# Mixing of a pair behind the next unit's scores, projections in front of both transposes: attention and feed-forward block on one core

## What is computed

```python
xn = layernorm(x)
q, k = rope(q, k)                       # q: 32 heads, k and v: 8 heads of 64
scores = einsum('bgrtd,bgsd->bgrts', q, k) / sqrt(64)
allowed = (j <= i) & (i - j < 128)
attn = softmax(where(allowed, scores, -inf))
out = einsum('bgrts,bgsd->bgrtd', attn, v)  @ Wo
ffn: fwht, W_up and W_gate, silu(gate) * up, fwht, W_down
return x + attention(xn) + ffn(xn)
```

## Time and profile before

| | us |
|---|---|
| median of 3 runs | 1280.19 (1279.04 to 1281.07) |
| the profiled execution | 1279.16 |
| span of its profile | 1277.4 |
| PE busy | 1251.5 (98%) |
| DVE busy | 904.4 (71%) |
| ACT busy | 779.6 (61%) |
| POOL busy | 644.0 (50%) |
| granted PE clock | 1.0 throughout |

### The profile page before, as it was taken

How to read it: one execution, slowest core, us unless ns; L and a number is a source line. 1 busy time by engine, 2 the same in 40 slices (tenths; PEclk the granted TensorE clock), 3 DMA queues, 4 the chain that set the end, 5 groups by cost and what they waited for, 6 DMA issues and landing times.

```text
span 1277.4 us, 38064 instructions
## 1 busy us (share of the span) xinstructions
PE 1251.5 (98%) x14574; PEld 1062.3 (83%) x14574; DVE 904.4 (71%) x1617; ACT 779.6 (61%) x2862; POOL 644.0 (50%) x655
## 2 busy tenths in 40 slices
PE   9999999999999999999999999999999999999997
PEld 5778888888888888878888888888888888888886
DVE  5678974788647885478855888458884588746875
ACT  3377762767528775377744867357672667626775
POOL 5346652466426654266641766327663376524663
PEclk9999999999999999999999999999999999999999
DMA  6415535144152442334332343314424145141431
GB/s 224 124 47 163 173 110 149 53 127 138 35 149 78 114 127 76 108 85 143 92 98 84 109 132 95 112 55 123 127 86 131 59 111 155 62 132 38 132 99 51
DMA packets 72354, 137.56 MB, mean 108 GB/s; under 512 B 15600, under 2 KB 29424, under 8 KB 72176
## 3 DMA queue, kind: packets, MB, share of 16 engines
q1 hardware_dynamic: 71040, 134.41, 35.1%
q10 hardware_dynamic: 1136, 0.73, 0.2%
HBM read 72.17 MB, written 12.58 MB: 66 GB/s over the span
## 4 chain that ended last, share of the span: by engine, by line
PE 82%; ACT 6%; SPq 4%; DVE 3%; DMA 2%; issue 2%; POOL 1%; DVEq 0%; POOLq 0%
PE PROJ L964 15%; PE PROJ L966 14%; PE PROJ L965 14%; PE S L1120 10%; PE TR L1134 8%; PE O L1151 5%; PE O L1163 4%; PE TR L1151 4%; ACT e_sb L643 4%; PE S L964 2%; SPq L397 2%; PE S L965 2%; PE S L966 2%; DMA q_stack<-qy 1%; SPq L387 1%
## 5 line engine op out<-in xcount | busy, mean ns | idle before, releaser
L643 ACT ACTIVATE e_sb<-S,negmax 128x128 f32<-128x128 f32 x1024 | 364.8, 382 | 25.0 <-DVE negmax L888 22.6
L511 POOL TENSOR_TENSOR e_sb<-e_sb,rinv 128x512 f32<-128x512 f32 x256 | 264.8, 1040 | 49.3 <-DVE rinv L893 49.0
L519 POOL TENSOR_SCALAR_AFFINE_SELECT p_cur<-pt_sb 128x512 f32<-128x512 f32 x192 | 122.5, 641 | 246.3 <-ACT pt_sb L653 246.3
L653 ACT ACTIVATE pt_sb<-TR 128x512 f32<-128x512 f32 x256 | 154.9, 605 | 135.7 <-PE TR L1134 135.4
L773 DVE TENSOR_TENSOR prod<-PROJ,rope_sb 128x1024 f32<-128x1024 f32 x160 | 193.3, 1212 | 60.0 <-PE PROJ L966 43.3
L643 ACT ACTIVATION_READ_ACCUMULATOR e_sb<-S,negmax 128x1 f32 x1024 | 225.3, 220 | 0.0
L888 DVE TENSOR_REDUCE negmax<-S 128x4 f32<-128x512 f32 x256 | 177.1, 692 | 8.9
L1120 PE MATMUL S<-k_stack,q_stack 64*64 64x64 f32 (+2 forms) x5632 | 180.2, 266 | 1.3 <-ACT e_sb L643 1.3
L487 POOL TENSOR_TENSOR qy<-prod 128x512 f32<-128x512 f32 x64 | 82.2, 1284 | 174.4 <-DVE prod L773 162.2
L1120 PEld LDWEIGHTS S<-k_stack,q_stack 64*64 64x64 f32 x5632 | 161.7, 133 | 8.6 <-ACT e_sb L643 5.4
L637 ACT ACTIVATE staging_rest<-PROJ,scale_gu_sb 128x512 f32<-128x512 f32 x64 | 44.2, 690 | 201.1 <-PE PROJ L966 201.1
(11 more groups left out here) (105 smaller groups left out, 2900.0 us busy)
## 6 DMA issues: line engine op xcount, KB each, us to landing
q_stack<-qy SPq DMA_DIRECT2D x512, 64.0 KB, 2.1
wq_ring<-wq_split_d SPq DMA_DIRECT2D x56, 512.0 KB, 4.7
wo_ring<-wo_split_d SPq DMA_DIRECT2D x56, 512.0 KB, 3.6
k_stack<-ky SPq DMA_DIRECT2D x256, 64.0 KB, 2.8
x_in<-x SPq DMA_DIRECT2D x8, 512.0 KB, 4.5
wq_split_d<-wq_ring SPq DMA_DIRECT2D x8, 512.0 KB, 4.3
wo_split_d<-wo_ring SPq DMA_DIRECT2D x8, 512.0 KB, 3.7
out<-acc SPq DMA_DIRECT2D x16, 256.0 KB, 4.3
```

The lines of the kernel that those rows point to most:

```text
L511: nc.gpsimd.tensor_tensor(e, e, r, ALU.mult).then_inc(norm_done, 1)
L643: last = nc.scalar.activation(e_sb[:, n % 2, r, :], s_heads(n, 1)[:, r, :], ACT.Exp, bias=negmax[:, n % 2, r:r + 1], accum_out=rowsum[:, n ...
L653: nc.scalar.activation(pt_sb[:, n % 4, :, :], TR[:, :, :], ACT.Copy).then_inc(t_copied, 1)
```

## The change

Four things change together.

1. PE: the mixing of pair u-2 stands behind the scores of unit u (before, the mixing of pair u-1 stood at the end of unit u). Both fillers now stand in front of the transposes they belong to: filler 2u, transposes 2u-2, filler 2u+1, transposes 2u-1.
2. ACT, DVE and POOL follow: o_copy(u-2) is the first of ACT's unit and exps stand before the copies; both folds come before o_low; mask(2u-3) follows normalise(2u-1), and mask(2u-2) follows the rotations.
3. `e_sb`, `rowsum` and `rinv` have four buffers instead of two, `pt_sb` two instead of four. t_copy(n) now waits for the mixing of pair n/2 - 1.
4. Two tables: the projection of the next row's first k moves from slots 25, 26 to 26, 27, and a `wo` product from slot 27 to 25.

```diff
-                  ... ("k", 0, NEXT): (25, 26), ("q", 0, NEXT): (28, 30)}
+                  ... ("k", 0, NEXT): (26, 27), ("q", 0, NEXT): (28, 30)}
+    WO_SLOTS[25] = WO_SLOTS.pop(27)
...
-        e_sb = sb("e_sb", [P, 2, REP, P])
-        pt_sb = sb("pt_sb", [P, 4, REP, P])
+        e_sb = sb("e_sb", [P, 4, REP, P])
+        pt_sb = sb("pt_sb", [P, 2, REP, P])
...
# POOL
                     if u:
                         normalise(2 * u - 1)
+                    if u >= 2 and (2 * u - 3) % TT:
+                        mask(2 * u - 3)
...
-                    for n in (2 * u - 2, 2 * u - 1):
-                        if n >= 0 and n % TT:
-                            mask(n)
+                    if u and (2 * u - 2) % TT:
+                        mask(2 * u - 2)
                     if u < UNITS - 1:
                         normalise(2 * u)
+                mask(STEPS - 1)
...
# ACT, t_copy
-                    if n >= 4:
-                        act.wait_ge(pv_done, b * STEPS + n - 3)
+                    if n >= 2:
+                        act.wait_ge(pv_done, b * STEPS + n // 2 * 2)
...
# ACT, the units
-                    if u:
-                        t_copy(2 * u - 2)
+                    if u >= 2:
+                        o_copy(u - 2)
...
                         exps(2 * u)
                     read_values(2 * u)
                     if u:
-                        t_copy(2 * u - 1)
+                        t_copy(2 * u - 2)
                     if u < UNITS - 1:
                         exps(2 * u + 1)
...
                     if u:
-                        o_copy(u - 1)
+                        t_copy(2 * u - 1)
...
# DVE
                         inverse_sum(2 * u - 1)
+                    if u < UNITS - 1:
+                        fold(2 * u)
+                        fold(2 * u + 1)
                     if u >= 2:
                         o_low(b, u - 2)
...
# PE
                         scores(2 * u)
                         scores(2 * u + 1)
+                    if u >= 2:
+                        values_mixed(b, u - 2)
+                    for n in (2 * u, 2 * u + 1):
+                        fill(n)
                         if u:
-                            transposes(2 * u - 2)
-                        fill(2 * u)
-                        if u:
-                            transposes(2 * u - 1)
-                        fill(2 * u + 1)
-                    else:
-                        for n in (2 * u, 2 * u + 1):
-                            fill(n)
                             transposes(n - 2)
-                    if 1 <= u < UNITS - 1 or b == BATCH - 1 and u:
-                        values_mixed(b, u - 1)
+            values_mixed(BATCH - 1, STEPS // 2 - 1)
```

More of the change, by code:

```diff
@@ L194, in attention_and_ffn_block @@
         negmax = sb("negmax", [P, 2, REP])
-        rowsum = sb("rowsum", [P, 2, REP])
-        rinv = sb("rinv", [P, 2, REP])
-        e_sb = sb("e_sb", [P, 2, REP, P])
-        pt_sb = sb("pt_sb", [P, 4, REP, P])
+        rowsum = sb("rowsum", [P, 4, REP])
+        rinv = sb("rinv", [P, 4, REP])
+        e_sb = sb("e_sb", [P, 4, REP, P])
+        pt_sb = sb("pt_sb", [P, 2, REP, P])
         p_cur = sb("p_cur", [P, 4, REP, P])
@@ L206, in attention_and_ffn_block @@
         h_sb = [p_cur[:, n, :, :].rearrange("p r q -> p (r q)") for n in range(2)]
-        down_stage = pt_sb[:, :, :, :].rearrange("p a r q -> p (a r q)")
+        down_stage = e_sb[:, :, :, :].rearrange("p a r q -> p (a r q)")
         wd_full = down_stage.rearrange("p (f c) -> p f c", f=FT)
@@ L508, in normalise @@
                     wait_apart(pool, "pool", rinv_done, b * STEPS + n + 1)
-                    e = e_sb[:, n % 2, :, :]
-                    r = rinv[:, n % 2, :].rearrange("p (r o) -> p r o", o=1).to_broadcast([P, REP, P])
+                    e = e_sb[:, n % 4, :, :]
+                    r = rinv[:, n % 4, :].rearrange("p (r o) -> p r o", o=1).to_broadcast([P, REP, P])
                     nc.gpsimd.tensor_tensor(e, e, r, ALU.mult).then_inc(norm_done, 1)
@@ L518, in mask @@
                         pool.wait_ge(pv_done, b * STEPS + n - 3)
-                    nc.gpsimd.affine_select(out=p_cur[:, n % 4, :, :], in_=pt_sb[:, n % 4, :, :], compare_op=ALU.is_ge,
+                    nc.gpsimd.affine_select(out=p_cur[:, n % 4, :, :], in_=pt_sb[:, n % 2, :, :], compare_op=ALU.is_ge,
                                             fill=0.0, base=0, pattern=[[0, REP], [1, P]],
@@ L642, in exps @@
                     for r in range(REP):
-                        last = nc.scalar.activation(e_sb[:, n % 2, r, :], s_heads(n, 1)[:, r, :], ACT.Exp,
+                        last = nc.scalar.activation(e_sb[:, n % 4, r, :], s_heads(n, 1)[:, r, :], ACT.Exp,
                                                     bias=negmax[:, n % 2, r:r + 1],
-                                                    accum_out=rowsum[:, n % 2, r:r + 1])
+                                                    accum_out=rowsum[:, n % 4, r:r + 1])
                     last.then_inc(exp_done, 1)
@@ L649, in t_copy @@
                     act.wait_ge(t_ready, b * STEPS + n + 1)
-                    if n >= 4:
-                        act.wait_ge(pv_done, b * STEPS + n - 3)
-                    nc.scalar.activation(pt_sb[:, n % 4, :, :], TR[:, :, :], ACT.Copy).then_inc(t_copied, 1)
+                    if n >= 2:
+                        act.wait_ge(pv_done, b * STEPS + n // 2 * 2)
+                    nc.scalar.activation(pt_sb[:, n % 2, :, :], TR[:, :, :], ACT.Copy).then_inc(t_copied, 1)
                 def o_copy(pair):
@@ L711, in _ @@
                     if u:
-                        t_copy(2 * u - 1)
+                        t_copy(2 * u - 2)
                     if u < UNITS - 1:
                         exps(2 * u + 1)
-                    if u == UNITS - 1 and b + 1 < BATCH:
-                        load_table(ACT.Silu)
                     read_values(2 * u + 1)
-                    if not u:
-                        value_mix(2)
                     if u:
-                        o_copy(u - 1)
-                    if u == 1:
-                        value_mix(3)
+                        t_copy(2 * u - 1)
+                    if u < 2:
+                        value_mix(u + 2)
+                if b + 1 < BATCH:
+                    load_table(ACT.Silu)
+                o_copy(STEPS // 2 - 1)
         @block.vector
@@ L809, in fold_low @@
                 ).then_inc(fold_lo, 1)
-            nc.vector.memset(e_sb[:, 0, :, :], 0.0).then_inc(warm_in, 1)
+            nc.vector.memset(p_cur[:, 2, :, :], 0.0).then_inc(warm_in, 1)
             row_stats(0)
@@ L892, in inverse_sum @@
                     dve.wait_ge(exp_done, b * STEPS + n + 1)
-                    nc.vector.reciprocal(rinv[:, n % 2, :], rowsum[:, n % 2, :]).then_inc(rinv_done, 1)
+                    nc.vector.reciprocal(rinv[:, n % 4, :], rowsum[:, n % 4, :]).then_inc(rinv_done, 1)
                 for j in HIDDEN_AFTER[0]:
@@ L937, in _ @@
                             x_low(b + 1, part)
-                    if u < UNITS - 1:
-                        fold(2 * u + 1)
                     for n in (2 * u, 2 * u + 1):
@@ L1045, in _ @@
             for n in range(3):
-                nc.tensor.matmul(S4[:, 3, :], e_sb[:, 0, 0, :], e_sb[:, 0, :, :].rearrange("p r q -> p (r q)"),
+                nc.tensor.matmul(S4[:, 3, :], p_cur[:, 2, 0, :], p_cur[:, 2, :, :].rearrange("p r q -> p (r q)"),
                                  start=True, stop=True)
@@ L1133, in transposes @@
                     for r in range(REP):
-                        last = nc.tensor.transpose(TR[:, r, :], e_sb[:, n % 2, r, :], ident[:, :])
+                        last = nc.tensor.transpose(TR[:, r, :], e_sb[:, n % 4, r, :], ident[:, :])
                     last.then_inc(t_ready, 1)
@@ L1151, in values_mixed @@
                                 last = nc.tensor.matmul(O_half[a][odd * D:(odd + 1) * D, s, :, :], v,
-                                                        pt_sb[:, (2 * pair + s) % 4, odd:REP:2, a * HP:(a + 1) * HP],
+                                                        pt_sb[:, s, odd:REP:2, a * HP:(a + 1) * HP],
                                                         start=s == 0, stop=False)
```

4 lines of the change are left out of this document (1 added, 3 removed).

## The result

| | before | after |
|---|---|---|
| median, us | 1279.62 (4 runs) | 1340.45 (1338.76 to 1341.78, 4 runs) |
| ratio | | 1.048, 95% interval 1.046 to 1.049 |
| span of the profile, us | 1277.4 | 1339.6 |
| PE busy, us | 1251.5 | 1280.3 |

The change costs 61 us; the prediction said 48 (1328, range 1296 to 1346).

The account below looks back on a forecast made before the run. PE, busy 1251.5 of 1277.4 us, was taken as the bound. Per row, 2.8 us of switches plus 6.5 of new waits minus 2.8 of old gave 6.5, 52 in eight; less 4, + 48: 1328 us, range 1296 to 1346.

Parts of the forecast that it names:

- The switches: PE changing tile shape between blocks: one more per inner unit, net 0.20 us a unit, 2.8 us a row, 22 in all.
- The unseen switch: PE going from 64x64 scores to the 128x128 mixing, absent from the trace: between 0 and 0.20 us, taken as 0.15.
- The 0.21 us "wait" of the transposes: First transposes of even units, said to wait for o_low: 0.21 us lost in units 2, 6, 8, 10 and 14.
- The wait for the mask: Even units 4, 6, 8, 10: step part waits 0.3 us for POOL's mask behind normalise, 1.2 us a row.
- wrong if even units are 6.35: Sign set beforehand: even units of 6.35 us, not 6.65, would mean the mask is in time and the sum wrong.
- The 2.8 us of old waits that go: PE's waits in the kernel before, in even units and units 3 and 11: 2.8 us a row, 22 in eight rows.
- the 4 us that the sum took off at the end: Taken off 52 us for the first row's unit 3 and last row's units 11 and 12, against a longer tail.
- Units 11 and 12: Waits around the transposes of x, x_high on ACT and the mask: together 1.7 us a row.
- Unit 14: Two products of 1.2 us ahead of step 27's reciprocal make the mask late: 0.8 us of wait.
- Unit 16: No scores there, so pair 14's mixing waits 0.8 us for a copy, plus 0.45 for mask(29): 1.25 us.
- the covered waits: Rival: switches are paid but most new waits stay covered; 24 us more, 1304 us (1290 to 1314), chance 0.22.
- The ring: Rival: the mask's chain from step part to step part bounds every unit, 7.4 us against 6.8; about 1358 us, chance 0.07.

Follow-up runs that it names:

- the version of the kernel before: Kernel before, with the first matmul of the filler put ahead of the transposes of even units: 1280.29 us, ratio 1.0010.

## Why the prediction came out as it did

**The switches: right in kind, a little too dear.** The count (one more in an inner unit) stands. The price was 0.20 and came out at 0.165 (18 us, not 22). The prediction's terms can be read in units 6 and 7, from the start of a block to the start of the next; nothing is late there but the step part of unit 6, which waits for the mask. For the kernel after the lines of units 6 and 7 above have the starts, for the kernel before, the product above (427.27) and these two:

```profile
429.11 0.36 PE L964 MATMUL PROJ<-wo_ring,o_hi 128*128 128x256 f32 x1
...
433.66 0.66 PE L1134 MATMUL TR<-ident,e_sb 128*128 128x128 f32 x4
```

| block, and what follows it before and now | predicted | before, us | after, us | measured |
|---|---|---|---|---|
| step part of 16 matmuls: scores, now a product | + 0.09 | 0.49 | 0.59 | + 0.10 |
| product of 6: transposes, now the same | + 0.11 | 1.48 | 1.51 | + 0.03 |
| transposes: a product, now scores | + 0.15 | 0.36 | 0.53 | + 0.17 |
| product of 12: mixing, now transposes | - 0.15 | 1.61 | 1.48 | - 0.13 |
| 48 scores: transposes, now mixing | 0 | 1.43 | 1.48 | + 0.05 |

The step that failed is the 0.11 added for the second matmul of a product: it is as late behind transposes (0.31), where the product stood before, so only 0.03 of the 0.11 came. The unseen switch, scores to mixing, was taken at 0.15, the same as the switch to transposes that it replaces. It is no cheaper: 1.48 us against 1.43 for 48 scores, 1.25 against 1.24 for 40. The first transposes of a unit win about as much, since they no longer stand behind scores (unit 6: 0.38 us before, 0.35 now). With the switch free, two inner units would be 0.10 us longer together by the prediction's terms; they are 0.33 longer. So it is not free, as the Trainium skill has it (TensorEngine Tiling (Array Packing), Key Properties); here the trace agrees.

**Even units: the right length from two errors.** The 0.21 us "wait" of the transposes was no wait (the version of the kernel before won nothing), so by the prediction's own terms an even unit without waits is 6.56 us long and not 6.35. The wait for the mask was counted at 0.3 and is 0.14. 6.67 came, 6.65 had been said: that is luck. The condition that the prediction set itself, "wrong if even units are 6.35", could not find this. Only the run that takes the mask out of the way did: 6.50 to 6.54.

**The 2.8 us of old waits that go: wrong.** 1.4 of it were these 0.21 and the 0.37 of unit 4, of which only some 0.12 was a wait (that version's unit 4 is 6.63 us long in the mean, 6.75 before). Another 0.5 a row was unit 3's. It had in fact 1.4 us in two rows and 0 to 0.7 in the others: POOL's rotation waits for a transfer there, and the mask stands behind it. In the kernel after, the rotation still waits, and now unit 4 pays (8.12 us in the row where unit 3 had 8.07). The same rotation in that row, before and after:

```profile
564.69 1.28 POOL L487 TENSOR_TENSOR qy<-prod 128x512 f32<-128x512 f32 x1 [2.44 <-DMA q_stack<-qy]
```

```profile
588.57 1.29 POOL L488 TENSOR_TENSOR qy<-prod 128x512 f32<-128x512 f32 x1 [1.78 <-DMA q_stack<-qy]
```

Added over the rows, unit 3 had 4.8 us over an undisturbed 6.59, and unit 4 now has 3.4 over 6.65. So the 4 us that the sum took off at the end, and a part of the 2.8, came back.

**The new waits.** Units 11 and 12: predicted + 1.22 for both against before; measured + 1.65 (7.65 + 7.48 - 6.44 - 7.04). Unit 10: predicted + 0.07; measured + 0.52. Both differences are DVE's x normalisation, which the walk along DVE did not have; the run that moves it gave 8.8 us, with units 10 and 11 shorter by 0.47 and 0.67. This is the omitted term. Unit 3: predicted 1.2 of wait; 7.96 - 7.00 gives 0.96. Here the named cause was right, two products behind a rotation. Unit 14: predicted + 0.57, measured + 0.59; its reciprocal comes at 499.94, 0.81 after the unit's start, and ends at + 0.98, for which + 1.0 had been said. Unit 16: the copy's 0.8 and the mask's 0.45 were 0.76 and 0.6.

**In sum**, by the prediction's own terms over eight rows: 0.2 us in six even units that could not be won, + 10; the mask in four even units at 0.14 instead of 0.3, - 5; switches, - 4; x normalisation, + 6 (by the unit lengths) to + 9 (by the run); the rotation's wait that moved, with the 4 us taken off, + 4 to + 6; unit 3, - 2. That is + 9 to + 14, against 13 missing. These pieces are read from unit lengths and partly estimated, so the sum shows that the terms suffice, not that each is exact. The chances: of the rivals, the covered waits (1304) have the number of the kernel with the mask in front and three halves of `prod`, by a coincidence: as it was run, the mask was late. The ring (1358) did not come: inner odd units are 7.00 and wait for nothing.

## What to carry to other kernels

An idle time before a weight load is a wait only if the matmul behind it is late too: lay a place with the suspected wait beside a similar one in which nothing can wait, and compare the ends of the matmuls before. When work is moved so that a chain just fits in one unit, walk every unit in which one of the chain's engines has extra work, and do it for the whole instruction list of that engine; the extra items cost nothing before the move and much of their length after. And before a wait is booked as a gain, ask for its cause in the row where it is longest: if that is a transfer, a new order of the engines moves it and does not remove it.

## What the runs showed of the hardware

- Two switches of the tile shape (128x128 to 64x64 and back) between transposes and a product cost PE 0.21 us. The order of an inner unit with one switch more costs 0.165 us more. A small matmul on 128x128 with 64 columns in fp32, with no switch, costs the path 0.18 us.
- The second matmul of a product (512 columns) starts 0.31 us after the first behind transposes, 0.32 behind a small matmul, 0.34 behind a switch; the third starts 0.23 to 0.24 after the second.
- Loads of 64x64 tiles end 0.34 us before their matmuls after 40 scores and 0.14 after 48, by the modelled ends of the matmuls.
- In the run with the transposes first, the granted clock was 0.50 in places, one of them after PE had stood still for most of 2.67 us, and 0.977 in the mean. In all the other profiled executions the mean was 0.999 to 1.0.
